# A post-layernorm decoder layer on one core: the quantised rows transposed by a DMA, and reordered products at the block borders

## The reference, cut to what matters

```python
x = layernorm(x + attention(x, Wq, bq, Wk, bk, Wv, bv))       # x is (2, 512, 1024)
x = layernorm(x + matmul(fake_quant(x), fake_quant(ctx)))     # ctx is (2, 1024, 1024)
x = layernorm(x + ffn(x))

def attention(x, ...):      # per token: 32 x 32 scores over the head dimension, not over tokens
    q, k, v = einsum('bse,edh->bsdh', x, W) + b               # k, v have 8 heads, repeated 4 times
    attn = softmax(einsum('bsdh,bseh->bsde', q, k) / sqrt(32))
    return einsum('bsde,bseh->bsdh', attn, v)

def fake_quant(x, s, z):
    return (clip(round(x / s + z), 0, 255) - z) * s

def ffn(x):                 # hidden 2048, latent 512, 8 experts
    h = relu(x @ up_w) ** 2
    moe = (x @ fc1_w @ expert_w) * sum(top_k(x @ gate_w, 2))
    return layernorm(h @ down_w + moe @ fc2_w, gamma, beta)
```

## Time and profile before

| | us |
|---|---|
| median of 3 runs (lowest, highest) | 638.35 (637.8, 639.55) |
| the profiled execution | 643.53 |
| its span | 641.7 |
| TensorE busy | 597.9 (93%) |
| VectorE busy | 379.6 (59%) |
| ScalarE busy | 299.4 (47%) |
| GpSimd busy | 121.3 (19%) |
| mean granted clock of TensorE | 0.979 of full speed |

### The profile page before, as it was taken

The page is one execution under the profiler, slowest core; times in us unless marked ns, Lnnn a source line. Parts: engine busy times, 40 slices in busy tenths (PEclk is TensorE's granted clock), DMA queues, the critical chain, the costliest instruction groups (busy, mean ns, idle before and its releaser), DMA issues.

```text
span 641.7 us, 9374 instructions
## 1 busy us (share of the span) xinstructions
PE 597.9 (93%) x3718; PEld 480.2 (75%) x3728; DVE 379.6 (59%) x514; ACT 299.4 (47%) x384; POOL 121.3 (19%) x162
## 2 busy tenths in 40 slices
PE   2799999898999799999999999998999999999991
PEld 1687877566776588788888888877888888888881
DVE  4937898889663373335333331419764565749875
ACT  4456687896693534333333331022344333314625
POOL 2811254635441042222110000000000000021000
PEclk9899999999999899999999999997999999999997
DMA  9766675583663868699799664003333336089903
GB/s 335 273 175 179 189 198 157 156 271 100 192 199 131 295 215 309 219 332 361 231 362 307 253 229 164 0 1 107 94 97 97 98 99 230 1 281 323 279 36 131
DMA packets 82108, 123.61 MB, mean 193 GB/s; under 512 B 23824, under 2 KB 50704, under 8 KB 82064
## 3 DMA queue, kind: packets, MB, share of 16 engines
q1 hardware_dynamic: 74592, 95.21, 44.4%
q0 software_dynamic: 5168, 19.40, 9.6%
q10 hardware_dynamic: 2304, 8.39, 4.0%
HBM read 83.13 MB, written 35.65 MB: 185 GB/s over the span
## 4 chain that ended last, share of the span: by engine, by line
PE 62%; DVE 4%; ACT 1%; issue 0%; DVEq 0%; ACTq 0%
PE psum L1547 32%; PE psum L1579 28%; PE psum L1505 0%; DVE stat_n L1901 0%; DVE x1T_lo L1770 0%; DVE ffn_lo L1920 0%; DVE ffn_hi L1920 0%; DVE ffn_hi L1909 0%; DVE ffn_lo L1909 0%; ACT x1T_hi L1616 0%; PE psum L1513 0%; PE psum L1514 0%; PE psum L1531 0%; DVE ffn_hi L1894 0%; ACT hx L1679 0%
## 5 line engine op out<-in xcount | busy, mean ns | idle before, releaser
L1774 DVE TENSOR_TENSOR u_lo<-u_raw,u_hi 128x1024 fp32r<-128x1024 f32 x18 | 23.8, 1320 | 84.3 <-ACT u_hi L1621 84.3
L1547 PE MATMUL psum<-x1T_hi,u_hi 128*128 128x512 f32 x160 | 63.4, 396 | 2.4 <-DVE x1T_lo L1770 2.4
L1547 PE MATMUL psum<-x1T_hi,u_lo 128*128 128x512 f32 x160 | 62.8, 392 | 0.0
L1547 PE MATMUL psum<-x1T_lo,u_hi 128*128 128x512 f32 x160 | 62.7, 392 | 0.0
L1579 PE MATMUL psum<-x2T_lo,x2T_hi 128*128 128x512 f32 x240 | 58.9, 403 | 3.1 <-DVE x2T_lo L1852 3.1
L1579 PE MATMUL psum<-x1T_hi,x2T_hi 128*128 128x512 f32 x264 | 61.5, 389 | 0.0
L1579 PEld LDWEIGHTS psum<-x1T_hi,x2T_hi 128*128 128x128 f32 x264 | 49.6, 188 | 10.3
L1579 PEld LDWEIGHTS psum<-x2T_lo,x2T_hi 128*128 128x128 f32 x240 | 47.0, 196 | 13.6 <-issue 3.5
L1547 PE MATMUL psum<-x2T_hi,u_hi 128*128 128x512 f32 x144 | 56.3, 391 | 0.0
L1547 PE MATMUL psum<-x2T_lo,u_hi 128*128 128x512 f32 x144 | 56.1, 389 | 0.0
L1547 PE MATMUL psum<-x2T_hi,u_lo 128*128 128x512 f32 x144 | 56.0, 389 | 0.0
(11 more groups left out here) (255 smaller groups left out, 1220.2 us busy)
## 6 DMA issues: line engine op xcount, KB each, us to landing
d_raw<-in_L_ffn_down_w_dram SPq DMA_DIRECT2D x20, 512.0 KB, 7.2
t_scratch<-d_raw SPq DMA_DIRECT2D x20, 512.0 KB, 5.8
d_raw<-t_scratch SPq DMA_DIRECT2D x20, 512.0 KB, 3.8
c_sb<-in_ctx_dram ACTq DMA_DIRECT2D x16, 512.0 KB, 3.6
u_raw<-in_L_ffn_up_w_dram SPq DMA_DIRECT2D x16, 512.0 KB, 5.2
r_scratch<-f1b SPq DMA_DIRECT2D x10, 512.0 KB, 5.3
r_scratch<-f2b SPq DMA_DIRECT2D x10, 512.0 KB, 4.6
x_sb<-in_x_dram SPq DMA_DIRECT2D x8, 512.0 KB, 5.2
```

What stands on the lines that cost most here:

```text
L1547: mm = pe.matmul(acc_b[:, q % 4], s, v, start=(k == 0 and i == 0), stop=(k == KT - 1 and i == 2))
L1774: dve.tensor_tensor(u_lo[:, m % 2], u_raw[:, m % 2], u_hi[:, m % 2].bitcast(F32), ALU.subtract).then_inc(S["u_lo_done"], 1)
```

## The change

There are four parts.

1. `transpose_q1` moves from TensorE to SP, as one DMA from `q1` to `q1T`; `q1T_out` of ScalarE goes. `quantise_b(t)` waits for the DMA of tile t - 1, `cross(t)` for that of tile t, for the evacuation of `cross(t - 1)` and, at t = 0 and 4, for `column_term`.
2. The lists of all five engines in the first block are written anew.
3. The second block begins with `first_products`: three transposes ahead in three banks, and three contraction steps of the second product between those of the first. `transpose_logits(0)` comes behind both. At the start of phase p1, `lo_out("p1", 0)` comes ahead of the last `latent`.
4. Phase p3 has five slots for `oa` (two of them in `oa_last`, which lies over `f2b0`), TAIL is 8 instead of 6, and the lists around it follow. The last row tile is normalised in two halves, by VectorE and ScalarE, and stored by SP and ScalarE.

```diff
+            def transpose_q1(t):
+                sp.wait_ge(S["q1_done"], t + 1)
+                if t >= 2:
+                    sp.wait_ge(S["xa_ready"], t - 1)
+                sp.dma_start_transpose(q1T[:, t % 2], q1[:]).then_inc(q1T_in[t % 2], 16)
...
             load_x(6)
             load_residual(3)
+            transpose_q1(0)
             ungroup(2)
+            regroup(4)
+            load_x(7)
             ungroup(3)
+            load_fc2(0)
+            transpose_q1(1)
             regroup(5)
-            load_fc2(0)
-            load_x(7)
             store_x2(0)
+            transpose_q1(2)
             regroup(6)
+            load_residual(4)
+            transpose_q1(3)
...
             def cross(t):
-                pe.wait_ge(S["q1T_done"], t + 1)
+                pe.wait_ge(q1T_in[t % 2], 16 * (t // 2 + 1))
+                if t >= 1:
+                    pe.wait_ge(S["xa_evac"], t)
+                if t % BT == 0:
+                    pe.wait_ge(S["col_done"], t // BT + 1)
...
             transpose_x(0)
+            transpose_x(1)
             project(0, 0)
-            transpose_x(1)
             project(0, 1)
             project(1, 0)
+            transpose_x(2)
             project(1, 1)
-            transpose_x(2)
             scores(0)
...
             scores(3)
+            column_sums(0)
             transpose_x(5)
-            column_sums(0)
+            cross(0)
+            values(3)
             project(5, 0)
-            transpose_q1(0)
-            values(3)
+            transpose_x(6)
             project(5, 1)
-            transpose_x(6)
-            cross(0)
             scores(4)
-            transpose_q1(1)
             project(6, 0)
             project(6, 1)
             cross(1)
             values(4)
             scores(5)
-            transpose_q1(2)
             transpose_x(7)
             cross(2)
-            project(7, 0)
-            transpose_q1(3)
             scores(6)
-            project(7, 1)
             cross(3)
             values(5)
+            project(7, 0)
+            project(7, 1)
             transpose_expert(0)
             transpose_expert(1)
             column_sums(1)
             values(6)
             transpose_expert(2)
             transpose_expert(3)
-            transpose_q1(4)
             scores(7)
             cross(4)
...
                 if t >= 1:
-                    act.wait_ge(S["q1T_ready"], t)
+                    act.wait_ge(q1T_in[(t - 1) % 2], 16 * ((t - 1) // 2 + 1))
...
-TAIL = 6
+TAIL = 8
...
+            def contraction(m, b, k):
+
+                st = [u[:, m % 2, k] for u in (u_hi, u_lo)]
+                for i, (s, v) in enumerate(split_products(st, (xT_hi[b][:, k], xT_lo[b][:, k]))):
+                    mm = pe.matmul(acc_b[:, product_index(m, b) % 4], s, v, start=(k == 0 and i == 0), stop=(k == KT - 1 and i == 2))
+                return mm
+
+            def first_products():
+
+                for k in range(3):
+                    transpose_x1(k)
+                pe.wait_ge(S["u_lo_done"], 2)
+                for k in range(KT):
+                    pe.wait_ge(S["x1T_lo_done"], k + 1)
+                    mm = contraction(0, 1, k)
+                    if k < 3:
+                        contraction(1, 1, k)
+                    if k + 3 < KT:
+                        transpose_x1(k + 3)
+                mm.then_inc(S["op_used"], 1)
+                for k in range(3, KT):
+                    mm = contraction(1, 1, k)
+                mm.then_inc(S["op_used"], 1)
...
-            transpose_x1(0)
-            transpose_x1(1)
-            product(0, 1)
+            first_products()
             transpose_logits(0)
-            product(1, 1)
...
                 if m >= 2 * UP:
-                    for b in range(BATCH):
-                        latent(m, b)
+                    latent(m, 0)
+                    if m == MU - 1:
+                        lo_out("p1", 0)
+                    latent(m, 1)
...
+        def oa_slot(s):
+
+            first = step("p3", 0)
+            if s < first:
+                return s % RD
+            return RD + s - first if s < first + 2 else s - first - 2
...
-                act.activation(ffn[i], ffn[i], ACT.Identity, bias=nbias[:, n:n + 1], scale=rstd[:, 1, n:n + 1]).then_inc(S["out_done"], 1)
+                cols = slice(BANK if n == TILES - 1 else 0, EMB)
+                act.activation(ffn[i][:, cols], ffn[i][:, cols], ACT.Identity, bias=nbias[:, n:n + 1],
+                               scale=rstd[:, 1, n:n + 1]).then_inc(S["out_done"], 1)
...
+            dve.wait_ge(S["nb_done"], TILES)
+            dve.tensor_scalar(ffn[order[-1]][:, 0:BANK], ffn[order[-1]][:, 0:BANK], rstd[:, 1, TILES - 1:TILES], nbias[:, TILES - 1:TILES],
+                              ALU.mult, ALU.add).then_inc(S["half_done"], 1)
...
```

More of the change, by code:

```diff
@@ L288, in _ @@
             regroup(7)
+            store_x2(3)
             load_fc2(3)
[L290 to L291 removed]
+            transpose_q1(4)
             load_xk(0)
[L293 removed]
             load_xk(1)
             load_residual(6)
+            load_gate()
             load_xk(2)
[L297 to L304 removed]
+            ungroup(6)
+            load_xk(3)
+            transpose_q1(5)
+            load_residual(7)
+            load_xk(4)
+            ungroup(7)
+            load_xk(5)
+            load_u(0)
+            store_w2(0)
+            transpose_q1(6)
+            load_xk(6)
+            store_x2(4)
             load_u(1)
             store_w2(1)
[L307 removed]
             load_xk(7)
+            transpose_q1(7)
             store_w2(2)
[L310 removed]
             store_x2(5)
@@ L372, in values @@
                 mm.then_inc(S["av_ready"], 1)
-            def transpose_q1(t):
-                pe.wait_ge(S["q1_done"], t + 1)
-                if t >= 1:
-                    pe.wait_ge(S["xa_evac"], t)
-                if t % BT == 0:
-                    pe.wait_ge(S["col_done"], t // BT + 1)
-                for k in range(KT):
-                    mm = pe.transpose(q1T_ps[:, k], q1[:, k * P:(k + 1) * P], so["ident_bf"][:])
-                mm.then_inc(S["q1T_ready"], 1)
             def column_sums(b):
@@ L535, in _ @@
             w2_product(7)
-            transpose_q1(7)
             transpose_x2(6)
@@ L742, in _ @@
-            cross_out(1)
+            xT_hi_out(7)
+            keys_diagonal(6)
+            x2_squares(1)
+            cross_out(2)
+            softmax_exp(5)
+            ctx_a(14)
             ctx_b(13)
-            q1T_out(2)
-            xT_hi_out(7)
-            x2_squares(1)
-            ctx_a(14)
             load_context(15)
-            quantise_b(3)
-            cross_out(2)
-            keys_diagonal(6)
+            normalise_x2(1)
+            x2_squares(2)
+            fc2_hi_out(0)
@@ L764, in _ @@
             expert_hi(1)
-            fc2_hi_out(0)
-            x2_squares(3)
+            quantise_b(4)
             fc2_hi_out(1)
-            normalise_x2(3)
-            quantise_b(4)
             keys_diagonal(7)
+            expert_hi(2)
             fc2_hi_out(2)
-            q1T_out(4)
-            expert_hi(2)
+            expert_hi(3)
             fc2_hi_out(3)
-            expert_hi(3)
-            cross_out(4)
+            x2T_hi_out(0)
             w2_out(0)
             softmax_exp(7)
+            quantise_a(5)
@@ L793, in _ @@
-            w2_out(4)
-            x2T_hi_out(3)
-            q1T_out(6)
             w2_out(5)
             normalise_x2(4)
-            split_u(0)
-            quantise_a(7)
             x2T_hi_out(4)
             x2_squares(5)
+            quantise_a(7)
+            split_u(0)
+            quantise_b(7)
             cross_out(6)
-            quantise_b(7)
             x2T_hi_out(5)
+            normalise_x2(5)
+            x2T_hi_out(6)
+            x2_squares(6)
+            x2T_hi_out(7)
             split_u(1)
-            q1T_out(7)
@@ L1301, in feed_forward @@
         xT_hi, xT_lo = [so["x2T_hi"], x1_hi], [so["x2T_lo"], x1_lo]
-        f1b0, f2b0, f1b1 = [sb(n, [P, NP, SEQ], F32) for n in ("f1b0", "f2b0", "f1b1")]
+        f1b0, f1b1 = [sb(n, [P, NP, SEQ], F32) for n in ("f1b0", "f1b1")]
+        with nc.sbuf_tensor("oa_last", [P, 8, SEQ], F32R) as oa_last:
+            pass
+        f2b0 = sb("f2b0", [P, NP, SEQ], F32)
         f2b1 = so["f2b1"]
@@ L1491, in _ @@
                 load_x2(n)
-            for n in range(TILES):
+            for n in range(TILES - 1):
                 i = order[n]
@@ L1542, in product @@
                 for k in range(KT):
-                    if b and m == 0:
-                        pe.wait_ge(S["x1T_lo_done"], k + 1)
-                    st = [u[:, m % 2, k] for u in (u_hi, u_lo)]
-                    for i, (s, v) in enumerate(split_products(st, (xT_hi[b][:, k], xT_lo[b][:, k]))):
-                        mm = pe.matmul(acc_b[:, q % 4], s, v, start=(k == 0 and i == 0), stop=(k == KT - 1 and i == 2))
-                    if (m, b) == (0, 1) and k + 2 < KT:
```

(9 more changed lines are left out.)

347 lines of the change are left out of this document (165 added, 182 removed).

## The result

| | before | after |
|---|---|---|
| median of the runs (us) | 639.15 (7 runs, 635.82 to 640.45) | 644.77 (7 runs, 642.1 to 648.54) |
| profiled execution, its span (us) | 643.53, 641.7 | 644.92, 643.1 |
| mean granted clock in it | 0.979 | 0.986 |
| second block's first transpose (us) | 209.88 | 216.78 |
| TensorE's last product ends (us) | 628.8 | 632.5 |

The changed kernel is slower: the ratio is 1.008, with a 95% interval of 1.0054 to 1.0106. The forecast was 633.6, and faster.

A forecast was written before the change was run, and what follows sets the result against it. The prediction took the first block to be bound by TensorE, so only its idle time, slow clock or lost work could pay. Terms -0.5 + 4.2 - 5.9 - 2.6 = -4.8 took 638.35 to 633.6 us, range 627 to 645.

The forecast's parts named there:

- the first block: Everything before the barrier: removed transposes and waits, new waits and opening, taken as -0.5 us, bounds -5 and +4.
- the replay: TensorE's new first-block list run with the old trace's durations and 5.0 us from q1_done to landing; gave -0.5 us.
- the opening: First block's start: transpose_x(1) ahead of project(0,0) makes TensorE stand until 22.1 us; +2.4 us, bounds +1 and +4.
- the new waits: First block: waits at tile 7's evacuation, context tile 15, scores(7), scores(6), cross(0), cross(3) and cross(4); +5.8 us.
- The first rival: First block: transposing DMA is slow, landing at 8 us or more, so cross products wait; +9, 642.6 us, chance 0.27.
- The second rival: First block: gain eaten, opening costs 4 us and new waits 2 more; near 638 us, chance 0.15.
- Removed: First block: eight transpose_q1 groups leave TensorE, -3.5 us, and the waits around them and ScalarE's copy, -4.4 us.
- Behind the barrier: Second block's start: product(2,0) waits 3.9 us for split_u(2) behind route(0), then slow clock +2.9; +4.2, bounds +1 and +6.
- Start of p1: Phase p1, near 432 us: early lo_out removes 3.1 us of wait and 2.8 of slow clock; -5.9, bounds -3 and -6.
- Tail: Kernel's end: VectorE's last tile starts at once, last normalisation halved, two smaller stores; -2.6 us, bounds -1 and -3.2.
- The second block's sum: Second block: border +4.2, start of p1 -5.9 and tail -2.6 us taken together, -4.3.
- From the profile to the median: Whole kernel: profiled execution 643.53 us, median 638.35, 5.2 less; differences from the trace were applied to the median.

The follow-up runs named there:

- e12: The changed kernel once more, unaltered, against the kernel before: ratio 1.0082, median 644.57 us.
- e9: Changed kernel with the transposing DMA of q1 replaced by an ordinary copy, so q1T isn't transposed: ratio 1.0067 to the kernel before, 643.26 us.
- e8: Changed kernel with the DMA transposes of q1 issued by ScalarE instead of SP: ratio 1.0109 to the kernel before, 648.12 us.
- e7: Kernel before, lists in old order, with q1 transposed by DMA issued from ScalarE: ratio 1.0048 to the kernel before, 643.79 us.
- e10: Changed kernel in its new order, but q1 transposed by TensorE and copied by ScalarE again: ratio 1.0213 to the kernel before, 652.91 us.
- e13: Kernel before with only the changed kernel's opening: ratio 1.0058 to the kernel before, 643.19 us.
- e15: Changed kernel with the old opening and split_u(2) ahead of route(0): ratio 0.9917 to the kernel before, 634.83 us.
- e5: First block of the kernel before, second block of the changed kernel with split_u(2) ahead of route(0): ratio 0.984 to the kernel before, 630.43 us.
- e17: Repeat of e5, old first block and new second block with split_u(2) ahead of route(0): ratio 0.9862 to the kernel before, 631.46 us.
- e3: First block of the kernel before joined to the second block of the changed kernel: ratio 0.9969 to the kernel before, 636.78 us.
- e4: Kernel before, lists in old order, with only the transposes of q1 done by DMA from SP: ratio 1.0364 to the kernel before, 663.74 us.
- e6: Changed kernel with tile 7 in the old order and VectorE's qkv_out(7) moved up to match: ratio 1.0227 to the kernel before, 653.31 us.
- e11: Changed kernel with both the old opening and the old order of tile 7: ratio 1.0142 to the kernel before, 647.68 us.
- e16: e15 with tile 7's old order and VectorE, ScalarE and GpSimd lists reordered to match: ratio 1.0062 to the kernel before, 643.74 us.
- e0: The kernel before once more, unchanged, for a second profile: 640.92 us (1 run), span 639.0.
- e1: Changed kernel with one line moved, split_u(2) ahead of route(0) on VectorE: ratio 0.9985 to the kernel before, 637.31 us.

## Why the prediction was wrong

**The step that failed** is the first block: "the replay itself gives -0.5 ... I take -0.5, with -5 and +4 as bounds at a landing of 5.0". It was +6.9 in the profiles (+6.0 with e12) and 7 to 9 us in the ratios, beyond the bound. Two of its terms were too small, the opening and the new waits, and the waits had a path that the sum left out: the place of the transposes in SP's own list. The first rival, a transfer that is slow because it transposes, was not the cause: the median from issue to landing was 4.6 us, and the plain copy of e9 gained nothing clear. The second rival came nearest. It had the opening at 4 us and more new waits, but ended at 638 and had a chance of 0.15. The terms:

- Removed: the transposes (4.9 us of busy time, taken as 3.5) and their waits of 4.4 went, as forecast.
- The opening, +2.4 with +4 as bound: measured 3.7 to 4.5. Right mechanism, mis-sized.
- New waits, +5.8: the profile shows 4.9 at q1T, 3.4 more at the keys, 1.5, 1.1 and 0.3 at smT, 11.2 us, and 1.7 us of slow clock at `cross(0)`, 12.9 in all. What was named was mostly right in size (1.1, 1.5 and 1.7 against 1.2, 1.1 and 1.8). Too small were `cross(0)` (0.5 forecast; 2.0 and 1.7), `cross(4)` and `cross(6)` (within 0.2 of the landing by the replay; 1.8 and 1.1), and `scores(6)` (0.8; 1.9). For the three at q1T there are two reasons, and both are in the 5.0 us from q1's end to landing that the replay used for every tile. At `cross(0)` and `cross(6)` the transfer itself was late, 6.4 and 6.0 us from an issue right behind q1: equal DMAs landed after 3.1 to 6.4 us, and where the slack is 0.2 us a late one is paid and an early one gives nothing back. At `cross(4)` the transfer took an ordinary 5.2, but SP issued it 2.7 us late; the same happened in e12 (2.0 late, 7.8 from q1's end, a wait of 1.6), and e8 shows the wait gone with the issue moved. Why the masks of `scores(6)` came late (1.9; at most 0.6 in e12) isn't shown.

One profile's waits are not a bill, though. In e12 the waits that were 11.2 are 7.8 and `cross(0)` runs at full clock, so 5.1 us less in all, and yet the block ended only 1.0 us sooner: the second x tile was waited for 1.1 us longer, and a slow stretch (0.96 over 120 to 160 us) stood elsewhere.

What e7, e10, e13 and e15 show together: 4 us of the loss are the opening; the DMA in place of TensorE is no gain in the old order (+3.1) and 8 us in the new one, at the places tried; e15, with the opening undone, is still 5 us behind e5 (0.9917 / 0.984 = 1.0078), or 3.6 behind its repeat e17. These lie among tile 7's waits, those for the transfer and the rest of the rewritten lists; how they divide stays open.

**Behind the barrier**, +4.2 of which 6.8 for the wait and the slow clock: the wait was 4.0 (3.9 forecast), the clock 3.0 (2.9; 1.6 to 3.0 over nine profiles), and moving one line gave 6.1, 6.8 and 8.3 us. Right in both. The sum was about 1 us too high: from the block's start to `product(2, 0)` it is 20.4 us against 20.2 before, so +3.2 with the clock.

**Start of p1**, -5.9: the wait of 3.1 went in every profile of the new second block. The 2.8 us of slow clock were in the profile of before but follow the same wait in only three of six profiles, so they were charged at about twice their mean (1.2 us over the six).

**Tail**, -2.6: 12.9 to 10.6 us, -2.3. Right.

**The second block's sum**, -4.3: e3 gave -2.0 (-3.3 to -0.7), the means over the profiles -3.8. The clock can explain part of the difference: 1.6 us at p1 alone.

**From the profile to the median.** The prediction took 5.2 us off both sides alike. But in 29 runs of the kernel before on one chip, a fit of time against mean clock gives 632.6 + 538 x (1 - clock), with a correlation of 0.9: at 0.979 it is 643.9, at the mean of 0.987 it is 639.7. The profiled execution was long because of slow stretches, and some of those were what the change was to remove.

## What to carry to other kernels

Price an overlap by the spread of the transfer, not by its median: a place in a hand-written order with 0.2 us of slack behind a DMA that lands in 3 to 6 us is a wait. Price it from the moment its data is ready, too, and look at what stands ahead of it in the list of the engine that issues it: one regroup of eight DMAs held a transfer back by 2.7 us. In lists kept by several engines, moving a step on some of them asks for a look at all: four of the attempts here (e4, e6, e11, e16) lost 8 to 23 us to another engine's list, each time a wait for something late with unrelated work queued behind it. (The moved `route(0)` touched one list and gained 6 to 8 us.) And split a change at its natural border before judging it: the second block with one line moved is 1.4 to 1.6% faster than the kernel before, and inside the whole change it was hidden by the first.

## What the runs showed of the hardware

A wait of 3.14 us was followed by a slow stretch in three profiles of six; behind the waits of 4.0 to 4.8 us at product(2,0), the granted clock fell in all nine profiles that have it (0.91 or 0.96 over 225 to 265 us). A transposing DMA of 256 KB from SBUF to SBUF holds the issuing queue 1.27 us (an ordinary one 0.52), from SP and from ScalarE alike (1.26), and lands after 3.0 to 8.6 us over all profiles (3.1 to 6.4 in the changed kernel's; the plain copy 2.4 to 6.8). Four one-column additions on VectorE took 1.98 us in one profile, 0.98 in the changed kernel's, 0.37 in e0, e4, e7 and e13, and 2.34 in e1. Behind a wait of 17.05 us pairs of products took up to 0.99 us instead of 0.51, in a window whose granted clock reads 1.00.
